# A causal attention and expert-routing block on one Trainium2 core: row sums issued behind the next values run, and the narrow diagonal score tiles of two heads scored together

## What is computed

```
q = _rotary(x @ Wq + bq); k = _rotary(x @ Wk + bk); v = x @ Wv + bv
logits = jnp.einsum('bqhgd,bkhd->bhgqk', qg, k) * scale
logits = jnp.where(causal, logits, jnp.float32(-1e+30))
w = jax.nn.softmax(logits, axis=-1)
out = jnp.einsum('bhgqk,bkhd->bqhgd', w, v).reshape(b, s, NQ * D)
return out @ Wo + bo
```

## Time and profile before

| | us |
|---|---|
| median of 3 runs | 1151.8 |
| lowest, highest | 1147.91, 1152.04 |
| the profiled execution | 1151.97 |
| its span, first to last instruction | 1150.4 |
| attention, first to last step on TensorE | about 43 to 996 |
| TensorE busy | 1070.4 (93%) |
| VectorE, GpSimd, ScalarE busy | 831.7, 588.4, 553.3 |

### The profile page before, as it was taken

The page is one execution under the profiler, slowest core; times in us unless marked ns, Lnnn a source line. Parts: engine busy times, 40 slices in busy tenths (PEclk is TensorE's granted clock), DMA queues, the critical chain, the costliest instruction groups (busy, mean ns, idle before and its releaser), DMA issues.

```text
span 1150.4 us, 16377 instructions
## 1 busy us (share of the span) xinstructions
PE 1070.4 (93%) x5471; PEld 652.4 (57%) x5471; DVE 831.7 (72%) x1948; ACT 553.3 (48%) x1155; POOL 588.4 (51%) x632
## 2 busy tenths in 40 slices
PE   4799999999899999998999999989999989897993
PEld 2456565554565555545555655455556454476992
DVE  5677878776778787767787877687877779763333
ACT  2444544545455455454545454545454345553551
POOL 5554655646356457473365673643544535435441
PEclk9789999999999999999999999999999989988997
DMA  8000000000000000000000000000020002502104
GB/s 235 18 1 1 1 1 1 2 1 1 1 1 1 1 1 1 1 1 1 1 1 1 1 1 1 1 1 1 1 74 1 1 1 91 141 26 81 31 25 123
DMA packets 30019, 25.07 MB, mean 22 GB/s; under 512 B 4481, under 2 KB 25345, under 8 KB 29937
## 3 DMA queue, kind: packets, MB, share of 16 engines
q1 hardware_dynamic: 26224, 18.45, 5.7%
q0 software_dynamic: 2272, 4.72, 1.2%
q10 hardware_dynamic: 1440, 0.85, 0.3%
HBM read 15.62 MB, written 8.40 MB: 21 GB/s over the span
## 4 chain that ended last, share of the span: by engine, by line
PE 73%; DVE 13%; issue 4%; POOL 3%; ACT 3%; DMA 2%; SPq 0%; ACTq 0%; DVEq 0%; POOLq 0%
PE PS L1539 19%; PE PS L1490 12%; PE PS L1521 11%; PE PS L1523 9%; PE PS L1623 3%; PE PS L1465 3%; PE PS L1500 2%; PE PS L1589 2%; PE PS L1472 2%; PE PS L1647 2%; PE PS L1563 2%; DVE full L1134 2%; DVE part_max L1109 2%; DVE PS L1112 1%; DVE full L1161 1%
## 5 line engine op out<-in xcount | busy, mean ns | idle before, releaser
L1109 DVE TENSOR_REDUCE part_max<-PS 128x1 f32<-128x512 f32 x384 | 258.8, 686 | 105.3 <-PE PS L1490 99.5
L879 ACT ACTIVATE full<-PS 128x512 f32<-128x512 f32 x384 | 222.7, 600 | 188.2 <-PE PS L1523 176.3
L1521 PE MATMUL PS<-store 128*128 128x512 f32 (+3 forms) x640 | 264.3, 413 | 3.1 <-ACT full L879 1.2
L1490 PE MATMUL PS<-store 128*128 128x512 f32 (+3 forms) x640 | 249.2, 417 | 8.4 <-ACT store L859 2.8
L1523 PE MATMUL PS<-store 128*128 128x512 f32 (+3 forms) x640 | 235.1, 367 | 0.0
L717 POOL TENSOR_TENSOR full<-full 128x512 f32<-128x512 f32 x120 | 156.0, 1330 | 130.2 <-PE PS L1539 129.2
L888 ACT ACTIVATE diag<-PS 128x512 f32<-128x512 f32 (+3 forms) x256 | 111.6, 442 | 196.2 <-PE PS L1526 158.8
L1490 PEld LDWEIGHTS PS<-store 128*128 128x128 f32 x640 | 118.3, 192 | 141.7 <-issue 49.7
L1539 PE MATMUL PS<-full,V 128*64 128x512 f32 x768 | 191.1, 608 | 0.0
L747 POOL TENSOR_TENSOR lower<-lower 128x320 f32<-128x320 f32 x64 | 60.7, 948 | 244.0 <-DVE lower L1093 241.7
L1521 PEld LDWEIGHTS PS<-store 128*128 128x128 f32 x640 | 122.4, 191 | 85.5 <-ACT full L879 24.6
(11 more groups left out here) (227 smaller groups left out, 1455.2 us busy)
## 6 DMA issues: line engine op xcount, KB each, us to landing
lower<-in_L_ffn_experts_w_dram SPq DMA_DIRECT2D x16, 256.0 KB, 3.9
sent<-full SPq DMA_DIRECT2D x1, 2574.0 KB, 12.2
full<-sent SPq DMA_DIRECT2D x9, 264.0 KB, 4.7
lower<-made SPq DMA_DIRECT2D x8, 256.0 KB, 5.0
full<-in_L_attn_x_dram SPq DMA_DIRECT2D x2, 512.0 KB, 7.1
out_dram<-XA SPq DMA_DIRECT2D x4, 256.0 KB, 2.8
made<-lower,back_to POOLq DMA_INDIRECT x39, 2.2
wo_sb<-in_L_attn_Wo_dram SPq DMA_DIRECT2D x1, 512.0 KB, 10.6
```

Source lines behind the costliest of these rows:

```text
L879: nc.scalar.activation(full[:, k % QUADS, r, :], PS[:, bank, :], ACT.Exp).then_inc(probs_ready, 1)
L1109: nc.vector.reduce_max(part_max[:, t, b:b + 1], PS[:, bank, 0:width], AX.X).then_inc(ring_dve, 1)
L1490: last = nc.tensor.matmul(PS[:, bank, 0:w], QT(ch % 2, h, t * P, (t + 1) * P), keys[:, 0], start=True, stop=True)
L1521: nc.tensor.matmul(o, keys[:, 0], QT(ch % 2, h, q0, BANK), start=True, stop=False)
```

## The change

Two things are changed. **The sums.** Once all steps have positions, `sums_behind_values` looks at each row sum except those of pairs 29 and 31, finds the next `pv` step at or behind it, and moves the row sum directly behind that, unless a score step that needs its quad comes first. The norm of that pair, and the output step of the chunk, are shifted by the same amount. 27 of the 31 row sums of this kind move. **The scores.** On the diagonal chunk, for r = 2 and r = 3 (256 and 128 columns), the two heads are one step: the same two float32r matmuls with both heads' queries as columns (512 and 256 wide), one mask matmul over both corners, and one exponential. 64 score steps fewer stand in the list.

```diff
+    def together(J, q, r):
+        return q == J % N_J // PAIRS and 2 * (TB - r) <= TB
...
-                main += [("s", J, q, r, 0), ("s", J, q, r, 1)]
+                main += [("s", J, q, r, 0)] + [("s", J, q, r, 1)] * (not together(J, q, r))
...
+        for x, p in at.items():
+            if x[0] == "rowsum" and x[1] not in (LAST - PAIRS, LAST):
+                behind = min(e for e in ends if e >= p)
+                if behind < wanted.get(x[1], behind + 1):
+                    shift[x[1]] = behind + 1e-6 - p
+        return [[(p + shift.get(x[1], 0.0) if x[0] in ("rowsum", "norm") else
+                  p + shift.get(x[1] * PAIRS + PAIRS - 1, 0.0) if x[0] == "out" else p, x) for p, x in items]
+                for items in placed]
+
+    steps += merge(*sums_behind_values(placed))
...
+                    if together(J, q, r):
+                        w = BANK - r * P
+                        nc.scalar.activation(diag[:, :, r, r * P:BANK],
+                                             PS[:, bank, 0:2 * w].rearrange("p (a n) -> p a n", a=2), ACT.Exp)\
+                          .then_inc(probs_ready, 1)
...
+                    if together(J, q, r):
+                        w = BANK - q0
+                        o = PS[:, bank, 0:2 * w].rearrange("p (a n) -> p a n", a=2)
+                        corner = o[:, :, 0:P]
+                        high, with_max = QT_rows(ch % 2)[:, J % PAIRS, :, q0:BANK], QMT_rows(J % PAIRS)[:, :, q0:BANK]
+                        mask = causal16[:, 1:2, :].broadcast_to([P, 2, P])
```

More of the change, by code:

```diff
@@ L97, in block_kernel, with score_step @@
     LAST = GROUPS * N_J - 1
+    def together(J, q, r):
+        return q == J % N_J // PAIRS and 2 * (TB - r) <= TB
+    def score_step(J, q, r, m):
+        return "s", J, q, r, 0 if together(J, q, r) else m
     def weight(x):
@@ L103, in weight @@
             part = 1.0 if b < J % N_J // PAIRS else ((t + 1) if x[0] == "max" else (TB - t)) / TB
+            if x[0] == "s" and together(J, b, t):
+                part *= 2
             return part * (3.78 if x[0] == "max" else 2.0)
@@ L259, in block_kernel, with local, quads_in, sums_behind_values @@
         placed.append(at)
-    steps += merge(*placed)
+    def local(J):
+        return J % N_J // PAIRS
+    QUADS = 7
+    def quads_in(order):
+        owners = []
+        for x in order:
+            if x[0] == "s" and x[3] == 0:
+                _, J, q, _, m = x
+                if q < local(J) or q == 0:
+                    owners += [(J, k, q) for k in range(2)] if together(J, q, 0) else [(J, m, q)]
+        return owners
+    def sums_behind_values(placed):
+        at = {x: p for items in placed for p, x in items}
+        ends = sorted({p for x, p in at.items() if x[0] == "pv"})
+        owners = quads_in([x for x in merge(*placed)])
+        wanted = {}
+        for old, (J, m, q) in zip(owners, owners[QUADS:]):
+            if old[2] >= local(old[0]) - 1 and q < local(J):
+                p = at["s", J, q, 0, m]
+                wanted[old[0]] = min(p, wanted.get(old[0], p))
+        shift = {}
+        for x, p in at.items():
[7 more added lines that the diff above has]
+    steps += merge(*sums_behind_values(placed))
+    quad_owner = quads_in(steps)
+    quad_of = {key: k for k, key in enumerate(quad_owner)}
     SCORES, RING, AV = 0, 2, 6
@@ L312, in emptied @@
             return self.engine_of[n], self.engine_of[:n + 1].count(self.engine_of[n])
-    def local(J):
-        return J % N_J // PAIRS
-    QUADS = 7
-    quad_of, quad_owner = {}, []
-    for x in steps:
-        if x[0] == "s" and x[3] == 0:
-            _, J, q, _, m = x
-            if q < local(J) or q == 0:
-                quad_of[J, m, q] = len(quad_owner)
-                quad_owner.append((J, m, q))
     def acc_quad(J, m):
@@ L398, in QMT, with QMT_rows @@
             return area[("QMT", "QMT_last")[h // 2]][:, h % 2 * BANK:(h % 2 + 1) * BANK]
+        def QMT_rows(j):
+            return area[("QMT", "QMT_last")[j]].rearrange("p (m n) -> p m n", m=2)
         FREE_SLOT = GROUPS * CHUNKS % KEY_SLOTS
@@ L719, in walk @@
                             continue
-                        pool.wait_ge(probs_ready, n.at["s", J, ch, TB - 1, m] + 1)
+                        pool.wait_ge(probs_ready, n.at[score_step(J, ch, TB - 1, m)] + 1)
                         acc = full[:, acc_quad(J, m)]
@@ L887, in exps @@
                     act.wait_ge(scores_ready, n.at[x] + 1)
-                    nc.scalar.activation(diag[:, m, r, r * P:BANK], PS[:, bank, r * P:BANK], ACT.Exp)\
-                      .then_inc(probs_ready, 1)
+                    if together(J, q, r):
[3 more added lines that the diff above has]
+                          .then_inc(probs_ready, 1)
+                    else:
+                        nc.scalar.activation(diag[:, m, r, r * P:BANK], PS[:, bank, r * P:BANK], ACT.Exp)\
+                          .then_inc(probs_ready, 1)
             def round_parts(x):
@@ L1509, in step @@
                     taken(("qmax", J, m))
+                    if together(J, q, r):
+                        taken(("qmax", J, 1))
                     before = n.scores_before(x)
@@ L1519, in step @@
                     bank = n.score_bank(x)
-                    o = PS[:, bank, q0:BANK]
-                    nc.tensor.matmul(o, keys[:, 0], QT(ch % 2, h, q0, BANK),
-                                     start=True, stop=False)
-                    last = nc.tensor.matmul(o, keys[:, 1], QMT(h)[:, q0:BANK],
-                                            start=False, stop=q < ch)
+                    if together(J, q, r):
+                        w = BANK - q0
[3 more added lines that the diff above has]
+                        mask = causal16[:, 1:2, :].broadcast_to([P, 2, P])
+                    else:
+                        o, corner, mask = PS[:, bank, q0:BANK], PS[:, bank, q0:q0 + P], causal16[:, 1, :]
+                        high, with_max = QT(ch % 2, h, q0, BANK), QMT(h)[:, q0:BANK]
+                    nc.tensor.matmul(o, keys[:, 0], high, start=True, stop=False)
+                    last = nc.tensor.matmul(o, keys[:, 1], with_max, start=False, stop=q < ch)
                     if q == ch:
-                        last = nc.tensor.matmul(PS[:, bank, q0:q0 + P], ident16[:], causal16[:, 1, :],
-                                                start=False, stop=True)
+                        last = nc.tensor.matmul(corner, ident16[:], mask, start=False, stop=True)
                     last.then_inc(scores_ready, 1)
@@ L1531, in step @@
                     ch = local(J)
-                    need(probs_ready, n.at["s", J, q, r, 1] + 1)
+                    need(probs_ready, n.at[score_step(J, q, r, 1)] + 1)
                     if q == 0 and r == 0 and J >= 2:
```

2 lines of the change are left out of this document (1 added, 1 removed).

## The result

The changed kernel takes 1161.8 us, median of 4 runs (1158.29 to 1164.34), against 1151.9 for the kernel before beside it. The ratio is 1.0092, with an interval of 1.0061 to 1.0123: it is slower by 0.9%, where I had forecast 1137.5 us and gave "slower" 4 in 100. The profiled execution is the fastest of the four (1158.29, span 1156.7), so what follows accounts for 6.3 of the 10 us; the other three had the same mean clock (0.963 to 0.965 beside 0.964) and took 2 to 6 us longer, and no profile shows why.

What follows compares the result with a forecast made beforehand. TensorE's own queue was taken as the bound. Savings of 6.9 + 2.6 + 7.7 = 17.2, less 4.4 lost, plus 1.8 of waits, gave 14.6 us off 1152.0; forecast 1137.5 us, 8-in-10 range 1130 to 1149.

Steps and rivals of the forecast that it cites:

- What bounds the kernel: Attention, about 100 to 990 us: TensorE's queue sets the time, its listed waits are small, VectorE is the second limit.
- Fewer changes between tiles: TensorE's runs of 64-column tiles fall from 246 to 223, at 0.30 us each: 6.9 us saved (5.1 to 8.1).
- r = 2: Merging two heads' 256-wide diagonal score tiles saves 0.08 us for each of 32 tiles: 2.6 us.
- r = 3: Merging two heads' 128-wide diagonal score tiles saves 0.24 us for each of 32: 7.7 us (2.2 to 11.2).
- the rival of the columns: Merged tiles stream no fewer columns, so merging's 10.3 us shrink to 1 or so: 1144.5 us, chance 0.10.
- the operand of two rows: Float32r matmul with two rows of queries: taken as free; rival price 0.11 on 128 matmuls, 14 us: 1151, chance 0.03.
- Where waits go: Turned maxima at pair 11's kind gain 2.0, row sums 0.7, starts of groups 1 to 3 lose 0.9: net 1.8 us gained.
- What doesn't come through: Savings lost: 1.1 us in the opening, 1.1 at the end, 2.2 in pairs where VectorE is at 90%: 4.4 us.
- VectorE's taking over: Rival: VectorE's queue sets the pace in half of the pairs, 8 us of savings go: 1148 us, chance 0.10.
- what would show the forecast: Signs in the later trace, among them pair starts closer by about 0.4 us each, evenly through the groups.
- The starved ring: Rival: joined row sums leave VectorE's ring of maxima empty, TensorE waits 0.8 us in 27 places: 1159 us, chance 0.04.

Runs made afterwards that it cites:

- experiment 10: Whole change, with maxima closed ahead of row sums 7, 15, 23 on VectorE and GpSimd summing pairs 8, 16, 24 before rotating a tile: 1149.0 us, 0.9987.
- after: The changed kernel with both parts of the change, against the kernel before: 1161.8 us, ratio 1.0092.
- experiment 3: Whole change, but row sums, norms and outputs of pairs 7, 15 and 23 stay where they were: 1150.9 us, 1.0005 of the kernel before.
- experiment 5: Whole change, but row sums, norms and outputs of pairs 6, 7, 14, 15, 22, 23 and 30 stay: 1143.9 us, 0.9941 of the kernel before.
- experiment 7: Whole change, maxima closed ahead of row sums 7, 15, 23 on VectorE, row sums of pairs 6, 14, 22, 30 left in place: 1153.4 us, 1.0025.
- the two fastest: Experiment 5, 1143.9 us; and experiment 10 with row sums of pairs 6, 14, 22 and 30 left in place, 1141.8 us, 0.9922.
- experiment 9: Experiment 5's kernel, with only the output product of chunks 3, 7 and 11 put where the whole change has it: 1150.0 us, 0.9997 of the kernel before.
- experiment 1: Narrow diagonal tiles of two heads scored together, every row sum, norm and output left in place: 1146.4 us, 0.9957 of the kernel before.
- experiment 8: Merging alone plus three unused VectorE reductions ahead of closing the maxima of pairs 4, 12, 20 and 28: 1156.1 us, 1.0056 of the kernel before.

## Why the prediction was wrong, point by point

**What bounds the kernel.** Right for the pace: TensorE's own queue sets it. But "an edit is worth what it takes out of TensorE's own queue" is the sentence that failed. It holds inside a stretch in which TensorE is never short of work. At the start of a group it has to wait for GpSimd and ScalarE (for VectorE in experiment 10), and there an item of its queue costs nothing, and taking it away gains nothing. The two waits that I listed, 8.1 and 2.5 us, were also not all: TensorE stood still for 27.2 us of the attention before.

**Fewer changes between tiles, 6.9 us.** Held: 6.3 with moving alone. In the row below row sum 10 stands in a values run and takes 0.95 (367.41 to 368.36) where the earlier trace rows has 1.01. The median of row sums went from 1.01 to 0.96; I had named 0.86 as what would be seen in a run, so most of the gain must lie in the neighbours.

TensorE after, pair 11, the merged groups (start to next start is what counts):

```profile
365.16 0.39 PE L1576 MATMUL PS<-store 128*128 128x512 f32 x1
...
365.74 0.81 PE L1510 MATMUL PS<-lower 128*128 128x384 f32 x2
...
367.41 1.03 PE L1615 MATMUL PS<-full,ones 128*64 128x512 f32 x4
368.36 0.38 PE L1576 MATMUL PS<-store 128*128 128x256 f32 x1
...
368.92 0.65 PE L1591 MATMUL PS<-diag,V 128*64 128x256 f32 x4
```

**r = 2, 2.6 us, and r = 3, 7.7 us.** Held in kind and nearly in size. Summed over all groups from the first matmul to the next instruction, r = 2 went from 24.5 us (64 groups) to 20.1 (32), 4.4 saved, and r = 3 from 23.1 to 15.4, 7.7 saved. Merging alone saved 8.9 of full-clock work. The merged groups took 0.58 (365.16 to 365.74) and 0.56 (368.36 to 368.92). So the rule that the prediction takes from the Trainium skill ("TensorE: Matmul & The Clock Gate", section "Back-to-back issue gap"), by which merging would be worth next to nothing, did not hold here, nor did the rival of the columns; and the operand of two rows shows no price. The groups' 12.1 us are more than the 8.9: some 3 us went to their neighbours, and no run shows which. The sum of savings, 17.2 by my count, measured 14.6.

**Where waits go, +1.8 us.** This is the first of two terms that failed: it measured -9.4. Its parts: the three waits at the group starts I sized at 2.0, and they measured 2.11, but I set them against 1.74 of before and stopped there. Three things near them I did not count: 0.46 new for a maximum at 299.25 and its likes, the turned keys' wait grown from 0.94 to 1.90 in pair 8's kind (experiments 3, 5 and 7 show it to be pair 6's move), and 0.97 new for VectorE's maxima at 332 us and its likes. These three are 2.4 us a group, some 7 us. A fourth is the wait of 1.68 at 104 us, 1.4 more than before, where the output product of chunk 0 was the filler; it stands in every kernel that moves the first pairs' row sums (1.66 to 1.68, and 2.67 with moving alone), the two fastest too. I had written that at these places "there are all scores and the output" behind the wait, and read that as harmless; the output was the filler (experiment 9). And merging has its own part of the waiting (4.7 us by itself, experiment 1); the prediction took only 2.2 us off for pairs in which VectorE is near its limit. The gains were real but small: 1.0 to 1.3 of the 2.0 at pair 11 and its likes, 1.6 of row sum waits.

**The clock, a term I did not have.** It measured -9.9 us. I took full clock as given, and had read the earlier trace rows wrongly: it is not 9 tenths or more through the whole attention, but 7 and 8 in the slices from 29 to 86 us and 8 in the one from 920 us on, and the first window of the earlier trace rows has 0.90. Only the middle was at full clock. The trace of before did show what a wait of 2 us can do, and I had passed over it, near the end of the attention (TensorE, then the windows behind each of the two):

```profile
918.21 2.05 PE L1589 MATMUL PS<-wo_sb,attnT 128*128 128x128 f32 x16 [1.96 <-DVE attnT L1177]
...
930.92 0.39 PE L1490 MATMUL PS<-store 128*128 128x256 f32 x1 [2.00 <-DVE part_max L1112]
```

```profile
931.30:934.70 3.40, 3.08 (x9) 1.87 (x7) 3.36 (x12) 2.37 (x3) 0.00 (x0) 0.50 0.01 2
918.20:921.60 3.40, 3.39 (x23) 2.85 (x25) 1.55 (x4) 0.84 (x2) 0.00 (x0) 1.00 0.02 5
```

Behind 2.00 us the clock fell, behind 1.96 it did not; no other wait of TensorE between 100 and 960 us was over 0.95. The change joined two waits of 0.83 and 0.91 into one that I had myself sized at 2.0. I should have priced that at some 3.4 us at half clock, 1.7 lost, in part of the places. That the waits bring the falls is shown by experiments 8 and 9, where nothing but a wait was added or a filler moved.

**What doesn't come through, -4.4 us.** The end shows 2.4 where I had 1.1, but that part varies by more than this with no edit in it (above). Pair 11 became 0.6 us longer (25.1 for 24.5) and pair 12 shorter by 2.4, so the sign that I had named for VectorE's taking over did appear. It doesn't mean that: TensorE stands still for only 0.1 us of pair 11 in after. Over pairs 10 and 11 it has 0.6 us less work and waits 0.9 longer, and the largest part of that is the 0.97 for VectorE's maxima. The savings are uneven, and not even, as I wrote under what would show the forecast. (The forecast's last step has a slip as well: 1137.4 less 0.2 is 1137.2, not 1137.5.)

**The rivals.** The starved ring (1159, chance 0.04) was the one with the right sign and nearly the right time, and by the wrong mechanism: it wanted 0.8 us in 27 places, and most of the loss is in seven: the second-last and last row sum of three groups, and the place at 104 us, doubled by the clock. VectorE does not take over in general; TensorE waits for it at pair 8 (1.90, through ScalarE) and at pair 10 (0.97), in each of three groups.

**What stays open.** What decides whether a wait of 2 us brings the clock down: experiments 8 and 9 show the same wait with both outcomes. Nor was it tried to leave only the end as it was (pair 30's row sum), or only the place at 104 us, so neither has an experiment of its own. And the waiting that comes with merging was not followed up.

## What to carry to other kernels

Before you move work out of a place on the busiest engine, ask what that place waits for if the work is gone: follow the wait two engines back (here TensorE to ScalarE to GpSimd), because behind the wait that the profile names there may be a second one that ends just as late. Two or three short waits with work between them were cheaper here than one of the same sum, since a stall of 1.7 us or more could also cost TensorE its clock for 3.4 to 6.8 us. And a rule applied to 27 places is worth timing with the ends of the loop left out: without the last two row sums of a group, the same change is 0.6% faster instead of 0.9% slower.

## What the runs showed of the hardware

Between 100 and 915 us, where TensorE is otherwise over 90% busy, the granted clock fell from 2.4 to 1.2 GHz (0.50 in the windows) for 3.4 or 6.8 us, during waits of TensorE or within 2.2 us of their end. These waits were of 1.66 to 1.68, 1.72, 1.75, 1.90, 2.11, 2.26 and 2.56 us. It did not fall at other waits of 1.66, 1.72, 1.75, 1.90, 2.26 and 2.56 us, nor at one of 2.67 with moving alone. In that stretch no fall stood at a wait of 1.42 us or less, in any of the fourteen traces. Near the end of the attention it also fell without a long wait just ahead (at 944.9 us before), so a single wait is not the only thing that brings it down. And a VectorE sum of two SBUF operands took 1.63 us instead of 0.69 while GpSimd summed, with GpSimd's four sums at 4.70 instead of 3.86.
